# Edge-softmax heads of a graph layer: a third pair of PSUM banks, the residual on GpSimd, the last tile's chain first, the next weights transposed ahead

## What is computed

```python
for h in range(Ws.shape[0]):                      # 8 heads of 64 features
    Wx = x @ Ws[h] + Wb[h]
    s = leaky_relu(Wx[v_tgt] @ a_w[h, :d] + Wx[v_src] @ a_w[h, d:] + a_b[h], 0.2)
    alpha = _segment_softmax(s, v_tgt, n)
    outs.append(segment_sum(alpha[:, None] * Wx[v_src], v_tgt))
...
x = x + _L0_gnn_ref(_layernorm(x), ...)           # "x2" in the kernel
# _L0_ffn_ref on _layernorm(x): the MEAN over all nodes picks one of 16 experts
scores = softmax(mean(x, axis=1) @ Wg + bg); idx = argmax(scores)
x = x + gate * (x_normed @ We[idx] + be[idx])     # "x3"
x = x + _L1_gnn_ref(_layernorm(x), ...)           # x_normed @ W.T + b, then aggregation
x = x + _L1_ffn_ref(_layernorm(x), ...)
```

## Time and profile before

| | before |
|---|---|
| median of 3 runs | 553.72 us (551.4 to 556.36) |
| the profiled execution, its own time | 548.52 us |
| its span in the trace | 546.8 us |
| TensorE busy | 487.1 us (89%) |
| VectorE busy | 437.4 us (80%) |
| ScalarE busy | 343.9 us (63%) |
| GpSimd busy | 69.6 us (13%) |

### The profile page before, as it was taken

The page is one execution under the profiler, slowest core; times in us unless marked ns, Lnnn a source line. Parts: engine busy times, 40 slices in busy tenths (PEclk is TensorE's granted clock), DMA queues, the critical chain, the costliest instruction groups (busy, mean ns, idle before and its releaser), DMA issues.

```text
span 546.8 us, 11526 instructions
## 1 busy us (share of the span) xinstructions
PE 487.1 (89%) x4388; PEld 356.0 (65%) x4389; DVE 437.4 (80%) x908; ACT 343.9 (63%) x659; POOL 69.6 (13%) x85
## 2 busy tenths in 40 slices
PE   0979999986689999999899889988899999999995
PEld 0756666664688888888677644544466587776662
DVE  8767777664999999995898778995787787887871
ACT  5366666657899999984665643344444558856820
POOL 3000000000000000000000020123334420321232
PEclk9989999998799999999999999999999999999998
DMA  6970000002011111102000069000001118966111
GB/s 153 354 258 1 1 2 1 2 2 100 2 50 50 50 50 49 50 4 78 1 1 0 2 221 337 1 0 2 3 21 42 59 60 298 373 237 215 62 54 54
DMA packets 25253, 45.11 MB, mean 82 GB/s; under 512 B 6962, under 2 KB 6998, under 8 KB 25197
## 3 DMA queue, kind: packets, MB, share of 16 engines
q1 hardware_dynamic: 23212, 39.16, 21.0%
q0 software_dynamic: 1952, 5.18, 2.6%
q10 hardware_dynamic: 32, 0.01, 0.0%
HBM read 33.23 MB, written 11.95 MB: 83 GB/s over the span
## 4 chain that ended last, share of the span: by engine, by line
PE 52%; DVE 33%; issue 8%; ACT 4%; DMA 2%; POOL 1%; ACTq 0%; SPq 0%; POOLq 0%; DVEq 0%
PE bank L1442 8%; PE bank L1832 6%; PE bank L1708 6%; DVE work L1125 4%; PE bank L1516 4%; PE bank L1468 4%; PE bank L1509 4%; PE bank L1803 3%; PE bank L1420 3%; PE bank L1611 3%; PE bank L1624 3%; DVE rings L1125 2%; DVE big L1235 2%; DVE st L887 2%; DVE work L1030 1%
## 5 line engine op out<-in xcount | busy, mean ns | idle before, releaser
L1611 PE MATMUL bank<-big,work 128*128 128x130 f16 x1080 | 67.4, 224 | 8.4 <-DVE work L1125 8.4
L1611 PEld LDWEIGHTS bank<-big,work 128*128 128x128 f16 x1080 | 64.3, 100 | 10.4 <-DVE work L1125 4.9
L1509 PE MATMUL bank<-big 128*128 128x180 f16 x320 | 58.1, 267 | 4.2 <-DVE big L988 4.2
L988 DVE TENSOR_TENSOR big<-mid 128x1024 f16<-128x1024 f16 (+1 forms) x88 | 59.8, 734 | 0.1
L685 ACT ACTIVATE mid<-aux,small 128x1280 f16<-128x1280 f32 x36 | 47.3, 1349 | 0.7 <-DVE work L1125 0.3
L1624 PE MATMUL bank<-big,mid 128*128 128x260 f16 x400 | 47.1, 275 | 0.1
L1708 PE MATMUL bank<-mid 128*128 128x512 f16 x200 | 47.2, 378 | 0.0
L586 ACT ACTIVATE mid<-bank 128x180 f32 x80 | 26.5, 331 | 28.9 <-PE bank L1516 28.1
L1624 PEld LDWEIGHTS bank<-big,mid 128*128 128x128 f16 x400 | 38.2, 96 | 7.5 <-issue 0.3
L1468 PE MATMUL bank<-big,rings 128*128 128x512 f16 x120 | 42.7, 378 | 0.1
L1509 PEld LDWEIGHTS bank<-big 128*128 128x128 f16 x320 | 35.6, 118 | 8.8 <-DVE big L988 5.9
(11 more groups left out here) (325 smaller groups left out, 1126.3 us busy)
## 6 DMA issues: line engine op xcount, KB each, us to landing
big<-in_L_ffn_W SPq DMA_DIRECT2D x10, 1024.0 KB, 9.0
mid<-in_L_ffn_W SPq DMA_DIRECT2D x6, 1024.0 KB, 14.4
xperm_scratch<-work SPq DMA_DIRECT2D x1, 5753.0 KB, 20.3
aux<-thr_scratch SPq DMA_DIRECT2D x8, 640.0 KB, 3.8
aux<-xperm_scratch SPq DMA_DIRECT2D x8, 523.0 KB, 4.3
row<-in_x SPq DMA_DIRECT2D x1, 2304.0 KB
aux<-in_L_gnn_Ws SPq DMA_DIRECT2D x4, 256.0 KB, 4.6
work<-in_L_gnn_W SPq DMA_DIRECT2D x1, 1024.0 KB, 6.6
```

Source lines behind the costliest of these rows:

```text
L988: return V.tensor_tensor(out.rearrange("p c (v two) -> p c v two", two=2), values.rearrange("p (v two) -> p v two", two=2).unsqueeze(1).to ...
L1509: mm(count_bank(base, k)[:, 0:RW], L_ring[:, slot, k * CH + j, :], R_ring[:, slot, k * CH + j, :], start=j == 0, stop=False)
L1611: ins = mm(acc_region(h, t), weighted[i % NC][:, t * P:(t + 1) * P], VP[:, s, part, h, :, :].rearrange("p b f -> p (b f)"), start=False, s ...
```

## The change

Five things are done. A third pair of banks, 6 and 7, takes the products of every third tile, so `all_edges(t)` waits for the heads of tile t-3. VectorE writes a tile's result into `share`, a buffer of two tiles, and for tiles 0 to 8 GpSimd adds it to x; the statistics of a tile come after the heads of the next one. For the last tile the order differs: the statistics of tile 8 come first, then the heads of tile 9 with the scale of tile 8 between them, then tile 9's addition on VectorE, its statistics and its scale, and only then the low half of tile 7. TensorE transposes three quarters of `gW` before it transposes tile 8, the last quarter after. ScalarE makes the high halves of the first two quarters after the last tile's norm, where it made them before that tile's square root.

```diff
+        share, _ = carve(mid, free0, [2, H, FE])
...
+        def edge_bank(t, g2):
+            return bank[(0, 2, 6)[t % 3] + g2]
...
+            for t in range(T - 1):                                   # GpSimd
+                g.wait_ge(sem("share_made"), t + 1)
+                xt = x[:, t, :].rearrange("p (h f) -> p h f", f=F)
+                nc.gpsimd.tensor_tensor(xt, xt, share[:, t % 2, :, 0:F], ALU.add).then_inc(sem("x2_made"), 1)
...
             for t in range(T):                                       # ScalarE
-                if t == T - 1:
-                    second_hi(0)
-                    second_hi(1)
                 ln_sqrt(T + t)
...
             act(gs[0:1, 6:7], ones[0:1, 0:1], ACT.Exp)
+            second_hi(0)
+            second_hi(1)
             a.wait_ge(sem("gate"), 2)
...
-            for t in range(T):                                       # VectorE
+            def heads_of(t, beside=None):
                 v.wait_ge(sem("U_done"), t + 1)
...
-                link(V.tensor_tensor(num[:, :, 0:F], num[:, :, 0:F], bc(rden, [P, H, F]), ALU.mult))
-                xt = x[:, t, :]
-                V.tensor_tensor(xt.rearrange("p (h f) -> p h f", f=F), xt.rearrange("p (h f) -> p h f", f=F),
-                                num[:, :, 0:F], ALU.add).then_inc(sem("x2_made"), 1)
-                v.wait_ge(sem("x2_made"), t + 1)
-                ln_stats(T + t, xt)
-                ln_scale(T + t)
+                V.tensor_tensor(sh[:, :, 0:F], sh[:, :, 0:F], bc(rden, [P, H, F]), ALU.mult).then_inc(sem("share_made"), 1)
...
+            heads_of(0)
+            for t in range(1, T - 1):
+                heads_of(t)
+                v.wait_ge(sem("x2_made"), t)
+                ln_stats(T + t - 1, x[:, t - 1, :])
+                ln_scale(T + t - 1)
+                if t >= 2:
+                    low_of(t - 2)
...
+            t = T - 1
+            v.wait_ge(sem("x2_made"), t)
+            ln_stats(T + t - 1, x[:, t - 1, :])
+            heads_of(t, lambda: ln_scale(T + t - 1))
...
+            ln_stats(T + t, x[:, t, :])
+            ln_scale(T + t)
+            low_of(T - 3)
...
             all_edges(0)                                             # TensorE
             all_edges(1)
             pe.wait_ge(sem("raw_made"), 4 * H)
-            for t in range(T):
-                if t < T - 1:
-                    tile_T(T + t, xh_ring[:, t % 2, :], bank[4 + t % 2])
-                if t + 2 < T:
-                    all_edges(t + 2)
-            second_weights()
+            all_edges(2)
+            for t in range(T - 2):
+                tile_T(T + t, xh_ring[:, t % 2, :], bank[4 + t % 2])
+                if t + 3 < T:
+                    all_edges(t + 3)
+            pe.wait_ge(sem("ld_gw"), 16)
+            pe.wait_ge(sem("U_used"), T - 1)
+            second_weights(0, K - 1)
+            tile_T(2 * T - 2, xh_ring[:, (T - 2) % 2, :], bank[4 + (T - 2) % 2])
+            pe.wait_ge(sem("U_used"), T)
+            second_weights(K - 1, K)
```

More of the change, by code:

```diff
@@ L1140, in _ @@
             v.wait_ge(sem("nacc_made"), H)
-            for t in range(T):
+            def heads_of(t, beside=None):
                 v.wait_ge(sem("U_done"), t + 1)
+                sh = share[:, t % 2, :, :]
                 for g2 in range(2):
                     hh = slice(4 * g2, 4 * g2 + 4)
-                    ins = V.tensor_tensor(num[:, hh, :], bank[2 * (t % 2) + g2][:, 0:4 * FE].rearrange("p (h f) -> p h f", f=FE),
+                    ins = V.tensor_tensor(sh[:, hh, :], edge_bank(t, g2)[:, 0:4 * FE].rearrange("p (h f) -> p h f", f=FE),
@@ L1147, in _ @@
                                           bc(A2[:, t, hh], [P, 4, FE]), ALU.mult)
                 ins.then_inc(sem("U_used"), 1)
+                if beside:
+                    beside()
                 v.wait_ge(sem("U_used"), t + 1)
-                link(V.tensor_tensor(num[:, :, :], num[:, :, :], nacc[:, t, :, :], ALU.add))
-                link(V.tensor_scalar(rden[:, :], num[:, :, F], 1e-30, None, ALU.max))
+                link(V.tensor_tensor(sh, sh, nacc[:, t, :, :], ALU.add))
+                link(V.tensor_scalar(rden[:, :], sh[:, :, F], 1e-30, None, ALU.max))
@@ L1160, in _, with low_of @@
-                if 1 <= t < T - 1:
-                    xT_low(T + t - 1, bank[4 + (t - 1) % 2], x2T[:, t - 1, :, :, :])
-                if t == T - 3:
+                V.tensor_tensor(sh[:, :, 0:F], sh[:, :, 0:F], bc(rden, [P, H, F]), ALU.mult).then_inc(sem("share_made"), 1)
+            def low_of(t):
+                xT_low(T + t, bank[4 + t % 2], x2T[:, t, :, :, :])
+            heads_of(0)
[6 more added lines that the diff above has]
+                    low_of(t - 2)
+                if t - 1 == T - 3:
@@ L1163, in _ @@
                     v.wait_ge(sem("deg_made"), T)
                     V.tensor_scalar(deg[:, :], deg[:, :], 1.0, None, ALU.add).then_inc(sem("dis"), 1)
-                if t == T - 1:
-                    v.wait_ge(sem("dis"), 2)
-                    V.reciprocal(dis[:, :], dis[:, :]).then_inc(sem("dis"), 1)
+            t = T - 1
+            v.wait_ge(sem("x2_made"), t)
+            ln_stats(T + t - 1, x[:, t - 1, :])
+            heads_of(t, lambda: ln_scale(T + t - 1))
+            xt = x[:, t, :].rearrange("p (h f) -> p h f", f=F)
@@ L1168, in _ @@
+            v.wait_ge(sem("share_made"), T)
+            V.tensor_tensor(xt, xt, share[:, t % 2, :, 0:F], ALU.add).then_inc(sem("x2_made"), 1)
+            v.wait_ge(sem("x2_made"), T)
+            ln_stats(T + t, x[:, t, :])
+            ln_scale(T + t)
+            low_of(T - 3)
+            v.wait_ge(sem("dis"), 2)
+            V.reciprocal(dis[:, :], dis[:, :]).then_inc(sem("dis"), 1)
             v.wait_ge(sem("xT_hi"), 2 * T - 1)
@@ L1471, in lin_a, with second_weights @@
                     ins.then_inc(sem("linA"), 1)
[L1473 to L1477, removed]
+            def second_weights(k0, k1):
+                for k in range(k0, k1):
                     for o in range(K):
@@ L1618, in all_edges @@
             def all_edges(t):
-                if t >= 2:
-                    pe.wait_ge(sem("U_used"), t - 1)
+                if t >= 3:
+                    pe.wait_ge(sem("U_used"), t - 2)
                 for g2 in range(2):
```

2 lines of the change are left out of this document (1 added, 1 removed).

## The result

| | before | changed |
|---|---|---|
| median | 551.89 us (20 runs, 549.67 to 556.36) | 548.26 us (20 runs, 546.21 to 552.91) |
| ratio of the runs | | 0.994, 95% interval 0.9917 to 0.9964 |
| the profiled execution, its span | 546.8 us, clock 0.985 | 550.4 us, clock 0.972 |

The change makes the kernel faster by 2.0 to 4.6 us. I had forecast 1.4 us and 552.3 us; the time lies under the stated range. A second measurement on one chip gave 549.22 us against 551.37 us, ratio 0.9949 (0.9923 to 0.9975).

A forecast was written before the change was run, and what follows sets the result against it. It took a round trip through four engines, 5.27 us a tile, to bound the stage. 2.1 us gained less 0.7 lost gave -1.4 us, scaled from 553.72 to 552.3 us; range 550.6 to 555.8, about 1 us of scatter below.

The forecast's parts named there:

- the moved copies: ScalarE's first two gW high halves, now before the gate's exponential, delay it 0.73 us; 0.7 us taken as lost.
- the head stage: The tile loop up to the last tile's statistics and scale: gives 2.1 us, or 3.1 without the wait for ScalarE.
- One tile of VectorE: VectorE's loop loses the 0.73 us residual addition and falls from 5.66 to 4.93 us a tile.
- one tile of TensorE: TensorE's floor is 5.14 us a tile; a two-tile round trip through four engines, 10.55 us, sets the pace at 5.27.
- Walking it through: Start times of passes and heads, tile by tile, to tile 9's multiplications, at 302.85 us and ending at 303.6.
- the stall: VectorE's wait inside tile 9's heads for ScalarE's square root for tile 8: 1.0 us.
- Tile 8's scale inside tile 9's heads: It waits for ScalarE, still queued on tile 7, so VectorE goes on at 304.6 instead of 303.6: 1.0 us.
- The third pair of banks: In the edge products on TensorE, it takes away the wait for the heads two tiles back.
- Parts costed at nothing: Tile 7's late low half (0.60 us), early gW transposes and FILL_A fit into existing waits; GpSimd's later streams are untouched.
- A: Rival, chance 0.15: only TensorE's floor and the heads count, no wait at tile 8, copies hidden; gain 3.1 us, 550.6.
- B: Rival, chance 0.12: GpSimd additions over rows of 64 take 2.2 us and hold nm; 2.1 us slower, 555.8.
- B's turning point: A GpSimd addition of about 1.8 us, where a 0.35 us hold in each round trip eats the 1.4 us gain.

The follow-up runs named there:

- on_dve: The changed kernel with all residual additions back on VectorE, GpSimd idle, order, banks and tail as changed; 552.04 us, ratio 1.0004 to the kernel before.
- sqrt8: The changed kernel with tile 8's square root ahead of tile 7's token sums on ScalarE; 547.83 us, ratio 0.9921 to the kernel before.
- hi_slot: The changed kernel with the high halves of gW's first two quarters made behind tile 8's norm on ScalarE; 548.67 us, ratio 0.9949 to the kernel before.
- two_pairs: The changed kernel with two pairs of banks for the edge products in place of three; 548.77 us, ratio 0.995 to the kernel before.
- pool2: The changed kernel with a second, unused GpSimd addition of the same size ahead of each residual addition; 551.71 us, ratio 1.0001 to the kernel before.
- before_again: The kernel before, unchanged, measured once more against itself; 551.00 us, ratio 0.9999.

## Why the prediction was wrong

The direction, the limits and the order of size were right; the time lies 4.0 us under the forecast of 552.3, of which

- 1.8 us is the base. I scaled from the median of the three runs shown, 553.72, and 20 runs have 551.89. I had written that the runs differ by 5 us and then took the middle of three as firm, with only 1 us of scatter at the lower end of the range. Against the base of 20 runs my forecast would have been 550.5.
- 1.1 us is the size of the gain: two terms of the sum, below.
- 1.1 us is left. The steps give 2.5 us, or 3.0 if TensorE does not feel the moved copies; the medians differ by 3.6 us, and the ratios of the two measurements stand for 3.3 (2.0 to 4.6) and 2.8 (1.4 to 4.2) us. The rest is inside the scatter, and I know of no mechanism for it.

So the steps that failed are three sizes: the 553.72 us that the gain was taken from, the 2.1 us of the head stage (2.9), and the 0.7 us of the moved copies (0.4).

Step by step:

**One tile of VectorE, one tile of TensorE.** Right. The pace is the round trip over two tiles, 10.46 us against 10.55 worked out, alternating as described, and neither VectorE's 4.93 nor TensorE's 5.14. The difference is in the step from head to statistics, 2.58 and not 2.66: the division signals another engine and VectorE goes on without waiting for it, 0.61 us behind the division's start where it was 0.72 with the wait (295.28 - 294.67 here, 292.11 - 291.39 in on_dve).

**Walking it through.** This step failed in size. I had the last statistics 52.4 us after the first head and they came at 51.57. Small excesses added up: 0.2 us in the first two heads (9.06 against 9.26), 0.25 in the six steps of the loop (31.85 against 32.1), 0.2 from tile 8's head to its statistics (4.90 against 5.1), 0.15 from there to tile 9's head (1.00 against 1.15), and 0.1 from tile 8's reciprocal to the last statistics; only the stall went the other way, by 0.1. The head stage gives 2.9 us where I had 2.1. A walk of ten steps should carry the unrounded differences of starts, not durations plus an allowance for signals.

**Tile 8's scale inside tile 9's heads.** Right: 1.10 us measured, 1.0 worked out, and shown to be the order of ScalarE by sqrt8, where it is gone.

**The moved copies.** The mechanism was right, the size not: "I take the full 0.7 us as lost", and it is 0.4 at the low half (hi_slot), perhaps less at TensorE. The two copies take 0.95 us beside the neighbouring operations in that place, not 1.11, and the expert's low halves did not wait in full behind the late exponential. I took the upper end of my range of 0 to 0.73 where a middle value was as good.

**The third pair of banks.** I credited it with taking away the wait for the heads two tiles back. two_pairs shows that the new order alone does that. The sum did not depend on it.

**Parts costed at nothing** held: L1197 (the former L1171) still waits 0.71 us behind the low half of tile 7, and TensorE's pause of 1.84 us ahead of tile 8's transposes, with the last quarter of gW and FILL_A behind it, ends before the last nm, for which TensorE then waits another 1.07 us.

**Rivals.** A, no stall and no cost of the copies, gives the measured size nearly (3.1 us), but by the wrong cause: both costs are there, under a larger gain of the stage. B's mechanism is real: pool2 shows the hold on nm. It does not occur in the changed kernel since an addition over rows of 64 out of 65 takes 1.18 us, 0.09 more than a contiguous one, and leaves 0.2 us of room. The 1.09 us was a lucky choice, though: it is nearly the shortest of the nine additions of its line, which take 1.08 to 2.09 us, 1.71 in the median. The six long ones (1.56 or more) all start while a VectorE operation with two SBUF inputs runs (last section). In the changed stage none runs beside the nine additions, and they take 1.17 to 1.19. B's turning point was put at 0.35 us of hold for a gain of 1.4, half of the hold on each of eight tiles; pool2's 0.63 us would give 2.5 by that rule and took 2.9 (54.52 against 51.57).

**What was not foreseen** is that a half-speed stretch can stand at the place from which I read the end of the chain. The one trace of before had none; nine of fourteen have (one of three of the kernel before, eight of the eleven others).

## What to carry to other kernels

When one engine's loop is the bound and another sits idle, moving a step pays only as far as the next limit, and that limit may be a round trip through several engines rather than any engine's load: add up one lap of it before and after. Putting work on GpSimd beside VectorE was free here while the addition ended before VectorE's next operation with two SBUF inputs, and none ran when it started; how small that operation is does not matter. Where the order of the last round differs from the steady one, look at what the other engines still have queued from the round before; here a few moved lines on ScalarE brought the last nm another 1.2 us forward. And the median of three runs that spread by 1% is no base for a range of 1%.

## What the runs showed of the hardware

- TensorE's granted clock falls to 0.50 (1.2 GHz) for some 3 us, in two traces some 10 us, in the gate chain or behind it, in nine of fourteen traces, one of three of the kernel before and eight of eleven of the others. Ahead of it TensorE has short products with pauses of 0.3 to 1.1 us between them, and with the new order 0.7 to 1.8 us at tile 8's transposes, where the kernel before has 0.5. Whether it falls is not decided by the kernel alone: before and before_again are the same program.
- A GpSimd addition of fp32 128x512 took 1.09 us over contiguous rows, 1.18 us with one input in rows of 64 out of 65, and 1.04 us when both inputs were the same tile, in such rows as its output.
- A VectorE operation of 128x1 with two SBUF inputs took 0.79 us beside a GpSimd addition and ended with it, where it takes 0.16 alone; statistics over 128x512 with one input kept 0.69 us.
- The hold works in the other direction too. In the kernel before a GpSimd addition started while VectorE was in an operation with two SBUF inputs, which ended at 388.08 us, and took 2.09 us, 1.12 of them behind that end, about its length alone; VectorE's next operation with two inputs, of 64x8, then took 1.22 us and ended with it:

```profile
385.79 2.29 DVE L1235 SCALAR_TENSOR_TENSOR big<-big 128x2048 f16<-128x2048 f32 x1
387.11 2.09 POOL L513 TENSOR_TENSOR row<-row,work 128x512 f32<-128x512 f32 x1 [3.39 <-ACT work L762]
387.99 1.22 DVE L1240 TENSOR_TENSOR pick<-ident 64x8 f16<-64x8 f16 x1
```
